# Moving a hand-written step schedule: first attention units fed through ScalarE's bias, and a layer norm spread block by block

## The reference, cut to what matters

```python
x = conv_attention(x)      # 2 images, 32x32 positions, 128 channels, 7x7 neighbourhood,
                           # 8 heads, gate, residual, then layer norm * ln_g + ln_b
t = x.reshape(2, 1024, 128)
n = (t - mean) / sqrt(var + 1e-5)                 # the second norm
q = n @ Wt ; k = n @ Wx                            # 32 features each
h = tanh(q[:, :, None, :] + k[:, None, :, :] + bh) # every query with every key
e = h @ Wa + ba ; a = softmax(e)
t = t + a @ n
t = t + expert_layer(norm(t))  # 8 experts, top 1, capacity 320, relu
```

## Time and profile before

| what | value |
|---|---|
| device time, median of 3 runs | 714.52 us (714.23 to 714.83) |
| the profiled execution's own time | 713.9 us |
| its span, first to last instruction | 712.1 us |
| busy: ACT, PE, DVE, POOL | 571.3, 548.5, 516.3, 506.1 us |
| tanh of all units (L1148), 128 instructions | 454.9 us |
| mean granted TensorE clock | 0.93 of 2.4 GHz |

### The profile page before, as it was taken

How to read it: one execution, slowest core, us unless ns; L and a number is a source line. 1 busy time by engine, 2 the same in 40 slices (tenths; PEclk the granted TensorE clock), 3 DMA queues, 4 the chain that set the end, 5 groups by cost and what they waited for, 6 DMA issues and landing times.

```text
span 712.1 us, 12354 instructions
## 1 busy us (share of the span) xinstructions
PE 548.5 (77%) x4512; PEld 272.0 (38%) x4512; DVE 516.3 (73%) x1442; ACT 571.3 (80%) x364; POOL 506.1 (71%) x588
## 2 busy tenths in 40 slices
PE   6997835999898969798939577676776666758994
PEld 3665621434343434354304122221231222237783
DVE  2677767877989797888865896977878778633456
ACT  3675637899999997999977999999999999920531
POOL 1002167997979778998998998989798798611474
PEclk9999975999999989899988899999999999977998
DMA  8600100100000000000800000000000000001400
GB/s 307 211 2 2 60 1 1 60 1 5 1 12 3 12 0 14 1 9 5 323 0 13 0 12 9 5 12 1 13 9 4 12 10 5 10 3 34 132 25 27
DMA packets 14108, 24.32 MB, mean 34 GB/s; under 512 B 1296, under 2 KB 11058, under 8 KB 13024
## 3 DMA queue, kind: packets, MB, share of 16 engines
q1 hardware_dynamic: 12640, 20.63, 8.5%
q0 software_dynamic: 1408, 2.91, 1.2%
HBM read 16.79 MB, written 7.37 MB: 34 GB/s over the span
## 4 chain that ended last, share of the span: by engine, by line
PE 32%; issue 21%; DVE 21%; ACT 17%; POOL 8%; DMA 1%; DVEq 0%; POOLq 0%; SPq 0%; ACTq 0%
ACT front L1148 15%; PE ps L895 9%; POOL front L581 5%; DVE front L1427 5%; PE ps L693 3%; PE ps L1056 3%; PE ps L1046 3%; PE ps L915 2%; DVE back L1236 2%; PE ps L722 2%; PE ps L741 2%; PE ps L732 1%; DVE back L1263 1%; POOL y_all L540 1%; PE ps L938 1%
## 5 line engine op out<-in xcount | busy, mean ns | idle before, releaser
L1148 ACT ACTIVATE front<-front 128x4096 f32<-128x4096 f32 x128 | 454.9, 3605 | 36.8 <-POOL front L581 24.9
L581 POOL TENSOR_SCALAR front<-k,q 128x1024 f32<-128x1024 f32 (+1 forms) x464 | 413.5, 908 | 42.3 <-PE ps L895 33.5
L895 PE MATMUL ps<-front,cst 128*32 128x512 f32 x2048 | 261.0, 630 | 80.4 <-ACT front L1148 73.5
L1427 DVE TENSOR_SCALAR front<-ps,q 128x512 f32<-128x512 f32 (+1 forms) x256 | 213.8, 878 | 22.0 <-PE ps L895 17.4
L895 PEld LDWEIGHTS ps<-front,cst 128*32 128x32 f32 x2048 | 55.9, 113 | 200.3 <-ACT front L1148 99.8
L1088 ACT ACTIVATE back<-back,mn 128x320 f32<-128x320 f32 (+1 forms) x128 | 62.4, 537 | 14.2 <-DVE mn L1236 14.2
L540 POOL TENSOR_SCALAR y_all<-y_all,mvs,lny 128x128 f32<-128x128 f32 x15 | 11.7, 786 | 74.2 <-DVEq L1392 58.9
L1236 DVE CUSTOM_DVE_ANT_0 back<-ps,back 128x320 f32<-128x320 f32 (+1 forms) x128 | 54.0, 469 | 12.5 <-PE ps L693 10.4
L1459 DVE COPY ptm<-ps 128x512 f32<-128x512 f32 x32 | 22.1, 692 | 38.2 <-PE ps L906 36.7
L693 PE MATMUL ps<-conv 32*128 32x320 f32 (+1 forms) x256 | 38.3, 477 | 4.9 <-DVE mn L1236 4.8
L1263 DVE COPY back<-ps 128x512 f32<-128x512 f32 x44 | 30.2, 686 | 7.5 <-PE ps L732 7.3
(11 more groups left out here) (146 smaller groups left out, 658.9 us busy)
## 6 DMA issues: line engine op xcount, KB each, us to landing
back<-in_w SPq DMA_DIRECT2D x2, 2048.0 KB, 10.8
xbuf<-rec SPq DMA_DIRECT2D x1, 2720.0 KB, 21.3
back<-in_top SPq DMA_DIRECT2D x2, 1024.0 KB, 6.2
back<-in_bottom SPq DMA_DIRECT2D x2, 1024.0 KB, 6.5
front<-xbuf SPq DMA_DIRECT2D x2, 720.0 KB, 7.0
back<-in_inner SPq DMA_DIRECT2D x1, 1280.0 KB, 10.6
back<-in_b SPq DMA_DIRECT2D x1, 1280.0 KB, 16.1
xT<-in_xT SPq DMA_DIRECT2D x4, 256.0 KB, 6.4
```

Of the source, the lines that this page charges most:

```text
L581: last = nc.gpsimd.tensor_scalar(ring[u % DEPTH][:, at + lo:at + hi], k4[:, img * L + k0 + lo:img * L + k0 + hi], q4[:, m:m + 1], 1.0, ALU ...
L895: last = nc.tensor.matmul(bank(to)[c * U:(c + 1) * U, :], c_("wa", U - QPG - QPG * row, 2 * U - QPG - QPG * row), ring[t % DEPTH][:, at:at ...
L1148: nc.scalar.activation(ring[t % DEPTH], ring[t % DEPTH], ACT.Tanh).then_inc(h_ready, 1)
L1427: last = nc.vector.tensor_scalar(ring[u % DEPTH][:, at + lo:at + keys], ps[:, base + k0 + lo:base + k0 + keys], q4[:, m:m + 1], None, ALU.add)
```

## The change

- In the 15th plain round (rho = 14) the tokens of blocks 0 to 3 are turned, instead of the 16th; ScalarE's copy follows the exponentials of that round. Query columns come before the last value products, keys of blocks 0 to 3 directly after them, in bank 2. The steps before t = 0 are gone: block 7's sums, spread and projection stand between the three products of the second image.
- Units 0 and 4 (`BIASED`) get no sums: ScalarE computes tanh(key + query) in eight instructions of 512 columns, with the query column as bias.
- VectorE and GpSimd have a written-out order up to step 1: units 1 to 3 between the norms of blocks 4 to 7. The first scale of blocks 4 and 5 is taken in round 14 (blocks 4 to 6 in round 15 before); blocks 6 and 7 are normed by VectorE (before, block 7 alone).
- Second norm, second image: blocks 8 to 11 keep their statistics at step 32 and their first chain at 33, but GpSimd takes one block in each of steps 34 to 37 and 42 to 45, weighs in 38 and 39, and the second chain is in step 41 (before: 39). Blocks 12 and 13 have chains in steps 44 and 48, block 14 in 50 and 52, block 15 in 54 and 55, all of block 15 by VectorE. The keys of blocks 12 to 15 are made in steps 56 to 58, and unit 64's sums in step 61 (before: 60 to 62, and 62).

```diff
-    gate = lambda u: FIRST if u < NEW_KEYS[1] else KEYS_1 if u < NEW_KEYS[2] else project_step(NB - 1) + 9
-    return [u for u in range(T) if max(u - DEPTH + 1, gate(u)) == t]
+    gate = lambda u: KEYS_1 if u < NEW_KEYS[2] else project_step(NB - 1) + 5
+    return [u for u in range(NEW_KEYS[1] + 1, T) if max(u - DEPTH + 1, gate(u)) == t]
...
+        rows_8, rows_12, rows_14, rows_15 = (project_step(j) + 1 for j in (11, 13, 14, 15))
+        SCALES = (0, 0, rows_8 + 1, rows_8 + 9, rows_12, rows_12 + 4, rows_14, rows_14 + 2,
+                  rows_15, rows_15 + 1)
...
 (TensorE, plain rounds and behind them)
-                if rho == RS - 1:
-                    pe.wait_ge(n_ready, NG * RS)
+                turn_probs(rho, 1)
+                if rho == RS - 2:
+                    pe.wait_ge(n_ready, NG * (RS - 1) + 1)
                     turn_tokens(0, 0)
-                turn_probs(rho, 1)
...
+            pe.wait_ge(n_ready, NG * RS)
+            query_columns(0, 1)
             values(RS - 1)
-            query_columns(0, 1)
+            key_half(0, 2)
+            sums(BS - 1)
+            query_key_rows("wqe", 2, 3, q_done)
+            spread(BS - 1)
+            pe.wait_ge(pta_ready, chunks_before(RS) - RS)
+            query_key_rows("wqo", 2, 4, q_done)
+            project(BS - 1)
             pe.wait_ge(ptd_ready, RS)
-            pe.wait_ge(pta_ready, chunks_before(RS) - RS)
-            key_half(0, 5)
-            query_key_rows("wqe", 2, 2, q_done)
-            query_key_rows("wqo", 2, 3, q_done)
-            query_key_rows("wk", 2, 4, k_done)
+            query_key_rows("wk", 2, 5, k_done)
...
 (ScalarE)
             def hidden_units(t):
-                act.wait_ge(pool_sums, t + 1)
-                act.wait_ge(dve_sums, t + 1)
+                if t in BIASED:
+                    n = BIASED.index(t) + 1
+                    act.wait_ge(k4_ready, n)
+                    act.wait_ge(q4_ready, n)
+                    if t >= DEPTH:
+                        act.wait_ge(h_used, t - DEPTH + 1)
+                    for at, k0, keys, m, _, _ in tiles_of_unit(t):
+                        last = nc.scalar.activation(ring[t % DEPTH][:, at:at + keys], k4[:, k0:k0 + keys], ACT.Tanh,
+                                                    bias=q4[:, m:m + 1])
+                    last.then_inc(h_ready, 1)
+                    return
...
 (VectorE, before step 1)
+            keys_out(0, 2)
+            inverse(BS - 1)
+            dve.wait_ge(ln_rows, 2)
+            dve.wait_ge(y_ready, 7)
+            row_stats(4, 7)
+            scaled(BS - 1)
+            key_query_sums(1)
+            gated(BS - 1)
+            dve.wait_ge(y_ready, BS)
+            row_stats(7, 8)
+            scale_late(0, 4, 8)
+            dve.sem_inc(ln_last, 1)
+            link.end()
+            normal_rows(y_all, 6, 8)
+            key_query_sums(2)
+            weigh_rows(6, 8)
+            row_stats(6, 8)
+            key_query_sums(3)
+            scale_late(0, 6, 8)
+            link.end()
+            normal_rows(x_all, 6, 8)
+            dve.sem_inc(t_ready[1], 1)
...
 (GpSimd)
+            key_query_sums(1)
+            key_query_sums(2)
+            normal_rows(2, 4, 6)
+            key_query_sums(3)
...
+                if rows_8 + 2 <= t < rows_8 + 6:
+                    scale_rows(3, t - rows_8 + 6, t - rows_8 + 7)
...
+                if rows_8 + 10 <= t < rows_8 + 14:
+                    normal_rows(3, t - rows_8 - 2, t - rows_8 - 1)
+                if rows_12 + 1 <= t < rows_12 + 3:
+                    scale_rows(4, t - rows_12 + 11, t - rows_12 + 12)
...
+                if t == rows_14 + 3:
+                    normal_rows(5, 14, 15)
...
 (VectorE, steps 44 to 55)
+                if t == rows_12:
+                    dve.wait_ge(misc_read, misc_uses(t))
+                    row_stats(12, 14)
+                    scale_late(t, 12, 14)
...
+                if t == rows_12 + 4:
+                    dve.wait_ge(ln_rows, 4)
+                    row_stats(12, 14)
+                    scale_late(t, 12, 14)
...
+                if t == rows_14:
...
+                if t == rows_14 + 2:
...
+                if t == rows_15:
+                    dve.wait_ge(misc_read, misc_uses(t))
+                    row_stats(15, NB)
+                    scale_late(t, 15, NB)
+                    link.end()
+                    normal_rows(y_all, 15, NB)
+                if t == rows_15 + 1:
+                    weigh_rows(15, NB)
+                    row_stats(15, NB)
+                    scale_late(t, 15, NB)
+                    link.end()
+                    normal_rows(x_all, 15, NB)
+                    dve.sem_inc(t_ready[3], 1)
```

More of the change, by code:

```diff
@@ L189, in sums_at, with summed @@
 def sums_at(t):
-    gate = lambda u: FIRST if u < NEW_KEYS[1] else KEYS_1 if u < NEW_KEYS[2] else project_step(NB - 1) + 9
-    return [u for u in range(T) if max(u - DEPTH + 1, gate(u)) == t]
+    gate = lambda u: KEYS_1 if u < NEW_KEYS[2] else project_step(NB - 1) + 5
+    return [u for u in range(NEW_KEYS[1] + 1, T) if max(u - DEPTH + 1, gate(u)) == t]
+def summed(u):
+    return u + 1 - sum(k <= u for k in BIASED)
 def leasts_before(n):
@@ L447, in keys_whole, with keys_bank @@
             return GROUPS[GROUP_AT[u]].half is None
-        KEYS_NEEDED = [1, 2, 4]
+        KEYS_NEEDED = {BIASED[0] + 1: 1, BIASED[1] + 1: 2, T // 2: 4}
+        def keys_bank(u):
+            g = GROUPS[GROUP_AT[u]]
+            return 2 * 512 if g.block >= BPI or g.half == 0 else 4 * 512
         def pool_part(u, n):
@@ L598, in scatter @@
                                              oob_is_err=False).then_inc(scattered[i % 2], 16)
-            for t in range(FIRST, END):
+            key_query_sums(1)
+            key_query_sums(2)
+            normal_rows(2, 4, 6)
+            key_query_sums(3)
+            for t in range(KEYS_1, END):
                 p = query_block(t, 12)
@@ L820, in turn_tokens @@
             def turn_tokens(half, to):
-                pe.wait_ge(t_ready[half], 2 if half == 1 else 1)
+                pe.wait_ge(t_ready[half], (1, 2, 4, 4)[half])
                 for k in range(4):
@@ L938, in keep_clock @@
                     nc.tensor.matmul(bank(3, 0, P), c_("ident"), c_("tri"), start=True, stop=True)
-            for t in range(FIRST, END):
+            for t in range(END):
                 rho = round_at(t, begin)
@@ L953, in _ @@
                     score_pair(rho, 1)
-                if t == FIRST:
-                    sums(BS - 1)
-                if t == FIRST + 1:
-                    spread(BS - 1)
-                if t == FIRST + 2:
-                    project(BS - 1)
                 rho = round_at(t, values_step)
@@ L1156, in soften_main @@
                 nc.scalar.activation(pm[:, lo:L], pm[:, lo:L], ACT.Exp, bias=nmin[:, :], scale=-1.0).then_inc(pm_ready, 1)
-            for t in range(FIRST, END):
-                if 0 <= t < T:
+            for t in range(END):
+                if t < T:
                     hidden_units(t)
+                if t == 0:
+                    query_rows(1, 0, 0, 3)
+                    query_rows(1, 0, 1, 4)
+                    act.wait_ge(k_done, 3)
+                    nc.scalar.activation(kT[:, 0:512], bank(5), ACT.Identity, bias=c_("bk")).then_inc(k_ready, 1)
                 p = query_block(t, 2)
@@ L1400, in _ @@
                     link.end()
-                if rho == 14:
+                if rho == 13:
                     dve.wait_ge(y_ready, 6)
                     row_stats(4, 6)
-                if rho == 15:
-                    dve.wait_ge(y_ready, 7)
-                    row_stats(6, 7)
-                    scale(4, 7, lnh[:, 4:7], lnw[:, 4:7])
+                if rho == 14:
+                    scale(4, 6, lnh[:, 4:6], lnw[:, 4:6])
                     dve.sem_inc(ln_scale, 1)
@@ L1411, in key_query_sums @@
             def key_query_sums(u):
-                g = GROUPS[GROUP_AT[u]]
-                img, half = g.block // BPI, g.half
                 if u >= DEPTH:
                     dve.wait_ge(h_used, u - DEPTH + 1)
-                if u in NEW_KEYS:
-                    dve.wait_ge(k4_ready, KEYS_NEEDED[NEW_KEYS.index(u)])
-                    dve.wait_ge(q4_ready, KEYS_NEEDED[NEW_KEYS.index(u)])
-                base = 5 * 512 if img == 0 else 2 * 512
-                if half is None and img == 0:
-                    base -= HL
-                if half == 1 and img == 0:
-                    base -= HL
+                if u in KEYS_NEEDED:
+                    dve.wait_ge(k4_ready, KEYS_NEEDED[u])
+                    dve.wait_ge(q4_ready, KEYS_NEEDED[u])
+                base = keys_bank(u)
                 for n, (at, k0, keys, m, _, _) in enumerate(tiles_of_unit(u)):
@@ L1562, in _ @@
                     bias_pair(rho, 1)
-                if t == FIRST:
-                    inverse(BS - 1)
-                if t == FIRST + 1:
-                    scaled(BS - 1)
```

(2 more changed lines are left out.)

130 lines of the change are left out of this document (51 added, 79 removed).

## The result

The changed kernel takes 723.24 us (median of four executions, 721.8 to 725.32) where the kernel before took 714.67 on the same chip: a ratio of 1.0119, 95% interval 1.0086 to 1.0152. A second series gave 723.43 against 715.52, 1.0100 (1.0072 to 1.0128). It is slower by 8 to 9 us (7.9 and 8.6), and the forecast was 709.5, at most 715.5. The profiled execution is the slowest of the first four, 725.32 us with a span of 723.5, so its times are some 2 us late.

The account below looks back on a forecast made before the run. ScalarE's tanh (454.9 of 712.1 us) were taken as the bound, with 36.8 us idle waiting for GpSimd and VectorE. 713.9 - 9 + 4 = 708.9, the median 0.6 above: 709.5 us, range 696.5 to 715.5.

Parts of the forecast that it names:

- Entry, 9 us: Start of the tanh: units 0 and 4 start earlier, gaining 9 us, bounds 5 and 12.
- Steps 33 to 43, 1 us: Norms of blocks 8 to 11: GpSimd scales a block while it used to wait, gaining 1 us, bounds -2 and 5.
- Steps 44 to 61: 4 us lost: Norms of blocks 12 to 15: more work on VectorE makes it late, 4 us lost, with the 1 us gain included.
- 3 of the 6.8 idle are filled, they take 63.4: Steps 44 to 55: 48.3 us plus 18.1 of VectorE work, less 3 of its 6.8 us idle, make 63.4.
- Rival 3: Steps 44 to 55: VectorE's six chains hold TensorE at bank 7, late loss 17 us, 722.5 us; chance 0.13.
- 380 on the old scale: Deciding sign for the slower case: step 55 ends past about 380 us, 69 us for 12 steps.
- Rival 1: Late steps: VectorE's lead hides its lateness, some 8 us around units 59 to 64 come back, 697.5 us; chance 0.24.
- Rival 2: Entry gives only 5 us as VectorE and GpSimd hinder each other, late loss 5, 714.5 us, no difference; chance 0.13.
- VectorE as releaser: Expected sign before units 48 to 60: ScalarE idle until VectorE, not GpSimd, releases it.

Follow-up runs that it names:

- the entry alone: Changed kernel with the second image's norms (blocks 8 to 15) and keys of blocks 12 to 15 as before: 708.4 us, ratio 0.9891 to the kernel before.
- the late spread alone: Kernel before with only blocks 12 to 15 normed in the new way: 731.99 us, ratio 1.0233 to the kernel before.
- entry with middle: Changed kernel with blocks 12 to 15 normed as before, blocks 8 to 11 in the new way: 708.91 us, ratio 0.9900 to the kernel before.
- the fourth corner: Changed kernel, hold at bank 7 kept, block 15's rows between scaling and norm in PSUM: 720.03 us, ratio 1.0052 to the kernel before.
- the four needless chains: Kernel before plus chains on unread numbers in steps 44, 48, 50, 52: 720.98 us holding TensorE at bank 7, 720.86 us with the last three in bank 3.

## Why the prediction was wrong

**Entry, 9 us: right.** 7.8 measured for the entry alone. The eight biased tanh took 5.01 us (4.9 forecast), VectorE's stretch from the gated block to the last norm 13.6 (98.94 to 112.52; 14.0 forecast), keys behind it 5.4 (5.55). Unit 0 was forecast for 92.9 and started at 95.56, because the plain rounds of this execution were late: with the same entry it starts between 92.89 and 95.82 in the other traces. Other profiled executions with the entry of before had unit 5 at 133.1 to 133.9 where it stood at 131.05 in mine, which makes the gain there 8.3 to 9.1. Missed was the wait of GpSimd for the energies of unit 1; the edit that takes it away gave 3.2 us more, of which the traces place 1.4 before unit 64.

**Steps 33 to 43, 1 us: none to be seen.** Inside its bounds (-2 to 5), and too small for these runs.

**"Steps 44 to 61: 4 us lost": the term that failed.** With the 1 us beside it, it stood for 5; measured are 14 to 17 (the late spread alone 16.7 by its ratio; after against entry with middle 1.0100 to 1.0119 against 0.9900, 14.3 to 15.7). Two steps of it failed.

First, "3 of the 6.8 idle are filled, they take 63.4", with step 55 at its end at 374.7. On that scale (unit 47 is 6.4 us ahead here) block 15's last row ends at 378.80 + 6.4 = 385.2. From unit 47 to 59 the step made 51.4 + 11 = 62.4 us, and it was 71.8. VectorE's added work was not undersized (18.1 forecast, 13.6 us busy measured). The sum let VectorE's idle time shrink by 3 us, and it grew by 6.8. What was put at nothing is that the added work comes in turns with TensorE's: TensorE waits at bank 7 for the chain, and VectorE behind the chain waits for the products that TensorE now has late. With the hold, the SBUF rows and the early tokens taken away (the run with later keys and rows in PSUM), and VectorE nearly as busy (52.66 us), the stretch from unit 47 to 59 is that of my sum (61.99 for 62.4), and the idle time has shrunk by 2.0 us (9.3 for 11.3):
```profile
308.98:370.97 61.99, 39.89 (x346) 18.11 (x350) 52.66 (x187) 46.21 (x16) 53.31 (x63) 0.90 0.24 94
```
So my sum was that of a kernel whose engines don't hold each other up.

Second, unit 64 was to follow unit 59 by 17.7 to 19 us, and it was 21.5. I had TensorE's energies of step 56 begin at 379, 62 us behind unit 47, and they began 70.5 behind it (382.14), at the low clock (3.64 us for 1.92), with four units of GpSimd's sums still to come. The two make 9.4 and some 3 us in this trace, where 9 to 12 were missing in the times.

Of the 15 to 16 us the ratios place: hold at bank 7 and block 15's rows in SBUF together 6.6 to 8 (1.0100 to 1.0119 against 1.0007), a division that the fourth corner leaves open; tokens and keys too early in TensorE's order 1.9 to 2.4 (1.0072 to 1.0038, 1.0007 to 0.9980); the rest, 5.7 (0.9980 against 0.9900), is what is left over. No run takes it away. That it is VectorE's own work is argued, from the last row above and from the 4.7 to 5.8 us of the four needless chains. These don't all add: with the others gone, no gain of two chains fewer is to be seen.

**The rivals.** Rival 3 named the size (17 lost, 722.5) and its deciding point, 380 on the old scale, was passed (385.2). Its mechanism was partly right. The hold is there in three rows of 2.9 to 3.8 us, and costs 2 to 3.4 us by the ratios, up to 7.4 by the traces. The low clock is there too (0.81 for 0.97 in the stretch), but in three units' energies of 3.33 to 3.64 us for 1.92, not behind all six chains; it is less when the waits are fewer (0.89 in the run with PSUM rows), and no run took it away by itself. I gave it 0.13 because I priced it as the coming together of two bad ends; the traces show one thing, engines that wait for each other. Rival 1 (VectorE hidden) fell. Rival 2 priced the slowing of VectorE's rows beside GpSimd at the entry, where it cost 1.4 us (rows of 1.06, 0.94 and 0.80 us for 0.60, 0.41 and 0.42), and not in step 54, where it cost 0.9 in the kernel after and 5.2 in the variants without the hold.

**What it would show.** VectorE as releaser was wrong by name: GpSimd's sums released ScalarE, behind TensorE, behind VectorE.

## What to carry to other kernels

When work is moved to an engine that is neither the busiest nor idle, sum the handovers as well as its time: find which other engine waits inside the same step and who waits behind that one. VectorE's idle time was no room to be filled here: part of it was waiting for TensorE, and it grew with the work. In a list of steps that each engine takes in order, one late operand (block 15) holds up all that stands behind it; move its consumer, too, and read what the wait becomes. Before two engines are given work in SBUF side by side, see whether an operand can be in PSUM.
